# Attention's maxima on a ring of four single banks, and key tiles shared out anew for the row sums

## The reference

```python
h = _ada_ln(x, cond, Wln1, bln1)
q, k, v = heads(h @ Wq + bq), heads(h @ Wk + bk), heads(h @ Wv + bv)
scores = einsum('bhqd,bhkd->bhqk', q, k) / sqrt(32)
attn = softmax(scores, axis=-1)
x = x + (einsum('bhqk,bhkd->bhqd', attn, v) reshaped) @ Wo + bo
h = _ada_ln(x, cond, Wln2, bln2)
x = x + gelu(h @ W1 + b1) @ W2 + b2
```

## Time and profile before

| | |
|---|---|
| median of three runs | 3452.63 us (3442.79 to 3455.45) |
| the profiled execution | 3454.36 us, its span 3453.1 us |
| busy over the span: PE, DVE, ACT, POOL | 96%, 58%, 41%, 42% |
| mean granted clock of PE | 0.978 of full speed |
| reductions of maxima in attention (L382) | 983, mean 1220 ns |
| adds on POOL (L791) | 192 of 4698 ns and 32 of 4576 ns |
| transfers into `accd` | 224 of 1024 KB |

### The profile page before, as it was taken

How to read it: one execution, slowest core, us unless ns; L and a number is a source line. 1 busy time by engine, 2 the same in 40 slices (tenths; PEclk the granted TensorE clock), 3 DMA queues, 4 the chain that set the end, 5 groups by cost and what they waited for, 6 DMA issues and landing times.

```text
span 3453.1 us, 43212 instructions
## 1 busy us (share of the span) xinstructions
PE 3312.9 (96%) x16794; PEld 2157.7 (62%) x16794; DVE 2008.8 (58%) x2541; ACT 1400.0 (41%) x2739; POOL 1466.8 (42%) x662
## 2 busy tenths in 40 slices
PE   8899999999999999999999997899999999999999
PEld 7677544445454454444444542778888888778888
DVE  4547767767677676777767771843333332226666
ACT  2121456656566565666656664311111111112222
POOL 0200667667676676767667675410000000002222
PEclk9999999999999999999999998999999999989999
DMA  5474567777877877778787766921111111201221
GB/s 196 142 221 136 148 173 174 182 176 175 192 178 171 184 171 175 183 173 185 172 188 179 176 153 161 310 72 37 37 37 37 37 37 52 86 33 61 71 74 56
DMA packets 186163, 466.20 MB, mean 135 GB/s; under 512 B 27076, under 2 KB 69308, under 8 KB 154215
## 3 DMA queue, kind: packets, MB, share of 16 engines
q0 software_dynamic: 32256, 234.90, 29.6%
q1 hardware_dynamic: 153703, 228.54, 22.2%
HBM read 151.94 MB, written 75.76 MB: 66 GB/s over the span
## 4 chain that ended last, share of the span: by engine, by line
PE 75%; DMA 13%; POOL 5%; DVE 3%; issue 2%; ACT 1%; SPq 0%; POOLq 0%; DVEq 0%; ACTq 0%
DMA accd<-pt 11%; PE ps L1089 10%; PE ps L1078 10%; PE ps L366 10%; PE ps L631 10%; PE ps L643 9%; PE ps L443 4%; POOL pacc L791 4%; PE ps L1609 3%; PE ps L649 3%; PE ps L1622 3%; PE ps L447 2%; PE ps L1642 2%; PE ps L1439 1%; PE ps L951 1%
## 5 line engine op out<-in xcount | busy, mean ns | idle before, releaser
L382 DVE TENSOR_REDUCE nmp<-ps 128x2 f32<-128x1024 f32 x983 | 1150.5, 1220 | 270.5 <-PE ps L366 269.5
L703 ACT ACTIVATE pt<-ps 128x512 f32<-128x512 f32 x2048 | 1037.5, 625 | 661.5 <-PE ps L631 656.2
L791 POOL TENSOR_TENSOR pacc<-pacc,pt 128x2048 f32<-128x2048 f32 x192 | 901.9, 4698 | 97.8 <-ACT pt L703 97.7
L631 PE MATMUL ps<-qs,ks 128*128 128x512 f32 x2048 | 781.3, 415 | 2.3 <-ACT pt L703 2.3
L366 PE MATMUL ps<-ks,qs 96*128 96x512 f32 x1966 | 749.5, 422 | 5.9 <-POOL ones L767 3.3
L366 PEld LDWEIGHTS ps<-ks,qs 96*128 96x128 f32 x1966 | 352.9, 189 | 297.3 <-DVE nmp L382 200.7
L631 PEld LDWEIGHTS ps<-qs,ks 128*128 128x128 f32 x2048 | 385.7, 189 | 205.7 <-ACT pt L703 144.3
L643 PE MATMUL ps<-pt,vq 128*32 128x512 f32 x4096 | 492.3, 598 | 0.0
L1078 PE MATMUL ps<-hpb,w 128*128 128x512 f32 x1536 | 383.0, 399 | 3.3 <-DMA x_d<-x 3.3
L1089 PE MATMUL ps<-w,gp 128*128 128x512 f32 x1536 | 380.5, 396 | 2.5 <-DVE gp L1222 2.5
L1089 PEld LDWEIGHTS ps<-w,gp 128*128 128x128 f32 x1536 | 289.4, 188 | 71.8 <-DVE gp L1222 2.9
(11 more groups left out here) (168 smaller groups left out, 3211.1 us busy)
## 6 DMA issues: line engine op xcount, KB each, us to landing
accd<-pt POOLq DMA_DIRECT2D x224, 1024.0 KB, 8.8
qk_d<-st SPq DMA_DIRECT2D x128, 256.0 KB, 2.7
ks<-qk_d SPq DMA_DIRECT2D x24, 1024.0 KB, 12.4
qs<-qk_d SPq DMA_DIRECT2D x96, 256.0 KB, 6.3
xina<-in_x SPq DMA_DIRECT2D x8, 1024.0 KB, 6.6
v_d<-vst SPq DMA_DIRECT2D x32, 256.0 KB, 2.4
vq<-v_d SPq DMA_DIRECT2D x8, 1024.0 KB, 12.2
recb<-r_d SPq DMA_DIRECT2D x32, 256.0 KB
```

The source lines that it names most:

```text
L382: dve.tensor_reduce(nmp[:, n // 4, n % 4:n % 4 + 2], ps[:, bank:bank + 2, :], AX.X, ALU.max, negate=True).then_inc(s_mr, 1)
L631: pe.matmul(ps[:, n % 3, :], ksb[w % 2][:, hh, 128 * kt:128 * kt + 128], qsb[:, v % 3, hh, :], start=True, stop=True).then_inc(s_sc, 1)
L703: act.activation(pt[:, g % 8, hh, :], ps[:, n % 3, :], ACT.Exp, scale=SCALE).then_inc(s_exp, 1)
L791: pool.tensor_tensor(pacc[:, :, :], first, pt[:, g % 8, :, :], ALU.add).then_inc(s_add, 1)
```

## The change

The four shared banks become a ring of single banks. A use waits for the use four before it. Each maximum matmul is signalled on its own and reduced on its own; maxima and scores alternate strictly. Tile 2 instead of 3 and so on goes by DMA: `ADD_DMA` is 1, 2, 4, 6, 8, 10, 12 and `ADD_POOL` 0, 3, 5, 7, 9, 11, 13, 14. `pe_sums` takes tile 15, slot 1 (last tile 10), `pacc`, slot 0 (last tile 12). `pool_values` moves from behind tile 10 to behind tile 9.

```diff
--- before.py
+++ after.py
@@ -32,13 +32,9 @@
 TRI = ((0, 0), (0, 1), (1, 0))
 HG = ((0, 6), (6, 5), (11, 5))
 EARLY = 84
-ADD_DMA = (1, 3, 5, 7, 9, 11, 13)
-ADD_POOL = (0, 2, 4, 6, 8, 10, 12, 14)
+ADD_DMA = (1, 2, 4, 6, 8, 10, 12)
+ADD_POOL = (0, 3, 5, 7, 9, 11, 13, 14)
 ADD_PE = (15,)
-
-ORDER = ("m", "m", "s", "m", "s", "m", "s", "s", "m", "s", "m", "s", "s", "m", "m", "s")
-
-
 def with_maxima(ci, j):
     return ci > NCH + 1 or (ci == NCH + 1 and j >= 8)
@@ -46,9 +42,7 @@
 def max_count(v, n):
-
-    u = 64 * v + n
-    return u + 1 if u < EARLY - 2 else (EARLY - 2) + (u - (EARLY - 2)) // 2 + 1
+    return 64 * v + n + 1
 def dma_count(v, kt):
@@ -73,16 +67,16 @@
             v, f = divmod(p, 8)
             if f == 6 and v + 1 < NU:
                 self.use(("row", v + 1))
-            for i in range(4):
-                if EARLY // 2 - 1 + 4 * p + i < 32 * NU:
-                    self.use(("max", EARLY // 2 - 1 + 4 * p + i))
+            for i in range(8):
+                if EARLY - 2 + 8 * p + i < 64 * NU:
+                    self.use(("max", EARLY - 2 + 8 * p + i))
             if f == 0 and v:
                 self.use(("sums", v - 1))
         self.use(("sums", NU - 1))
     def use(self, what):
-        self.bank[what] = 3 + 2 * (len(self.uses) % 2)
-        self.before[what] = self.uses[-2] if len(self.uses) > 1 else None
+        self.bank[what] = 3 + len(self.uses) % 4
+        self.before[what] = self.uses[-4] if len(self.uses) > 3 else None
         self.uses.append(what)
@@ -342,44 +336,40 @@
             for r in range(2):
                 sp.dma_start(qsb[96 + r:97 + r, v % 3, :, :].bitcast(F32), nmr[:, r, :].bitcast(F32)).then_inc(s_md, 16)
-        def pe_pair_free(what):
+        def pe_bank_free(what):
             if ring.before[what] is None:
                 return
             kind, n = ring.before[what]
             if kind == "max":
-                pe.wait_ge(s_mr, max_count(n // 32, 2 * (n % 32) + 1))
+                pe.wait_ge(s_mr, n + 1)
             elif kind == "row":
                 pe.wait_ge(s_nh, 2 * n + 2)
             else:
                 pe.wait_ge(s_accs, n + 1)
-        def pe_max(p, half):
-            v, n = p // 32, 2 * (p % 32) + half
+        def pe_max(u):
+            v, n = divmod(u, 64)
             w = v // NCH
             hq, kc = divmod(n, 4)
             if n == 0:
                 pe.wait_ge(s_qd[v % 3], 48 * (v // 3 + 1))
                 pe.wait_ge(s_kd[w % 2], 48 * (w // 2 + 1))
-            if half == 0:
-                pe_pair_free(("max", p))
-            m = pe.matmul(ps[:, ring.bank["max", p] + half, :], qsb[0:96, v % 3, hq // 4, 128 * (hq % 4):128 * (hq % 4) + 128],
-                          ksb[w % 2][0:96, hq // 4, CH * kc:CH * kc + CH], start=True, stop=True)
-            if half:
-                m.then_inc(s_mm, 1)
+            pe_bank_free(("max", u))
+            pe.matmul(ps[:, ring.bank["max", u], :], qsb[0:96, v % 3, hq // 4, 128 * (hq % 4):128 * (hq % 4) + 128],
+                      ksb[w % 2][0:96, hq // 4, CH * kc:CH * kc + CH], start=True, stop=True).then_inc(s_mm, 1)
         def pe_row(v):
             pe.wait_ge(s_nm, v + 1)
-            pe_pair_free(("row", v))
+            pe_bank_free(("row", v))
             pe.transpose(ps[0:16, ring.bank["row", v], 0:128], nm[:, :], ident[:, :]).then_inc(s_nt, 1)
-        def dve_max(p):
-            v, n = p // 32, 2 * (p % 32)
-            bank = ring.bank["max", p]
+        def dve_max(u):
+            v, n = divmod(u, 64)
             if n == 0:
                 dve.wait_ge(s_nm, v)
-            dve.wait_ge(s_mm, max_count(v, n))
-            dve.tensor_reduce(nmp[:, n // 4, n % 4:n % 4 + 2], ps[:, bank:bank + 2, :], AX.X, ALU.max,
+            dve.wait_ge(s_mm, u + 1)
+            dve.tensor_reduce(nmp[:, n // 4, n % 4:n % 4 + 1], ps[:, ring.bank["max", u], :], AX.X, ALU.max,
                               negate=True).then_inc(s_mr, 1)
         def sp_load_k(w, r):
@@ -652,14 +642,15 @@
         def pe_sums(v):
             bank = ring.bank["sums", v]
-            pe_pair_free(("sums", v))
+            pe_bank_free(("sums", v))
             for kt in ADD_PE:
                 pe_ones(bank, pt[:, (16 * v + kt) % 8, :, :], kt == ADD_PE[0], False)
-            for i in range(2):
-                pe.wait_ge(s_dma[i], dma_count(v, ADD_DMA[len(ADD_DMA) - 1 - (len(ADD_DMA) - 1 - i) % 2]))
-                pe_ones(bank, accd[:, i, :, :], False, False)
+            pe.wait_ge(s_dma[1], dma_count(v, ADD_DMA[-2]))
+            pe_ones(bank, accd[:, 1, :, :], False, False)
             pe.wait_ge(s_add, add_count(v, ADD_POOL[-1]))
-            pe_ones(bank, pacc[:, :, :], False, True).then_inc(s_end, 1)
+            pe_ones(bank, pacc[:, :, :], False, False)
+            pe.wait_ge(s_dma[0], dma_count(v, ADD_DMA[-1]))
+            pe_ones(bank, accd[:, 0, :, :], False, True).then_inc(s_end, 1)
         def pe_attention():
             qkv_over(pe)
@@ -669,16 +660,11 @@
                 v, f = divmod(p, 8)
                 if f == 6 and v + 1 < NU:
                     pe_row(v + 1)
-                ns = nm_ = 0
-                for what in ORDER:
-                    if what == "s":
-                        pe_scores(2 * p + ns // 4, ns % 4)
-                        ns += 1
-                    else:
-                        pair = EARLY // 2 - 1 + 4 * p + nm_ // 2
-                        if pair < 32 * NU:
-                            pe_max(pair, nm_ % 2)
-                        nm_ += 1
+                for i in range(8):
+                    u = EARLY - 2 + 8 * p + i
+                    if u < 64 * NU:
+                        pe_max(u)
+                    pe_scores(2 * p + i // 4, i % 4)
                 if p:
                     pe_values(2 * p - 2)
                     pe_values(2 * p - 1)
@@ -741,12 +727,12 @@
                     dve_row_split(v + 1, ring.bank["row", v + 1])
                 if f == 1 and v:
                     dve_sums(v - 1)
-                for i in range(4):
-                    pair = EARLY // 2 - 1 + 4 * p + i
-                    if pair < 32 * NU:
-                        dve_max(pair)
-                        if pair % 32 == 31:
-                            dve_row_max(pair // 32)
+                for i in range(8):
+                    u = EARLY - 2 + 8 * p + i
+                    if u < 64 * NU:
+                        dve_max(u)
+                        if u % 64 == 63:
+                            dve_row_max(u // 64)
                 if f == 2 and v:
                     dve_recip(v - 1)
                 if v == NU - 2 and f % 2:
@@ -789,7 +775,7 @@
                         pool.wait_ge(s_add, add_count(v, kt) - 1)
                         first = pacc[:, :, :]
                     pool.tensor_tensor(pacc[:, :, :], first, pt[:, g % 8, :, :], ALU.add).then_inc(s_add, 1)
-                if kt == 10 and v:
+                if kt == 9 and v:
                     pool_values(v - 1)
             pool_values(NU - 1)
```

## The result

The changed kernel takes 3343.22 us in the median of four runs (3338.52 to 3345.59) against 3451.37 of the kernel before: ratio 0.9688, 95% interval 0.9667 to 0.9710. I had said 3313, in a range of 3298 to 3360. The direction and the mechanism were right; a little over a fifth of the forecast gain (30 of 138 us) did not arrive. The profiled execution has a span of 3341.0 us against 3453.1.

What follows compares the result with a forecast made beforehand. Attention was taken as bound by PE, with its waits inside iterations and at unit ends to be won. 76 + 66 - 2 = 140 us off 3454.36 gave 3314, stated as 3313 us for the median; range 3298 to 3360.

Steps and rivals of the forecast that it cites:

- (1): Attention iterations: single-bank ring and alternating order cut the period from 6.12 to 5.81 us, 76 us over 246 iterations.
- (a): DVE reductions in attention don't overlap, each takes its whole 0.68 us: 42 us more, 3355 us; chance 12%.
- (c): Inside iterations, waits for exponentials replace those for maxima; period stays near 6.1 us, only sums gain: 3385 us; chance 4%.
- The 0.66 us of the Trainium skill: DVE's 512-element PSUM-to-SBUF reductions: by this estimate periods some 0.08 us longer, the run about 20 us above forecast.
- (2): Turning the row and copying the sums take one ring bank instead of two; taken as 0, with 10 us for the range.
- (3): New tile sharing at unit ends: 50.5 us of idle and 12 to 14 us of halved clock go, 66 us.
- its sentence on `pool_values`: On GpSimd, `pool_values` goes one tile earlier; the recip it waits for was in place long before.
- for which I left 2: Allowance of 2 us for remnants of waits near key loads, subtracted from the forecast gain.
- 0.9 us to spare: DVE's eight reductions take 4.9 us, hidden inside a period of 5.8, with 0.9 us left.
- (b): Iteration shrinks, but sums still wait, on `pacc` behind two adds or on tile 12: 3377 us; chance 7%.
- (d): Slot 0's chain, tiles 4, 8 and 12: slow landings make tile 12 late; 3630 us at 16.0 us each; chance 3%.
- (e): PE's clock falls inside iterations; one in eight at double length adds 180 us, 3493 us; chance 2%.

Runs made afterwards that it cites:

- the runs of the two halves: Old interleaving on single banks, against the changed kernel: 3383.44 us; strict alternation on pairs of banks, against the kernel before with only the new tile sharing: 3457.68 us.

## Why the prediction was right, and where not

- **Period** (1). 5.81 us forecast, 5.77 to 5.82 measured; reductions 0.60 apart; no wait for ACT or DVE inside. The 0.66 us of the Trainium skill (VectorE: DVE Perf Modes, the section on the TRN2 errata) was not what these instructions took: 0.68 us for one alone, 0.60 from one to the next. Rivals (a) and (c) are out. With the runs of the two halves, the layout on which it rested (where a load falls due, when its bank is free) gave 6.0 to 6.1 and 6.3 to 6.5 for 6.11 and 6.41: it can be trusted to a tenth of a microsecond.
- **Row and sums on one bank** (2). I took 0. A clean unit fell by 2.94 us where eight iterations of 0.31 give 2.48, some 12 us over the run that I had not counted. The iteration with the row went from 6.36 to 5.87 us and the one with the sums from 9.69 to 9.25, the others from 6.12 to 5.79 or so: about 0.3 us a unit belongs to the row and the sums, the rest to a period slightly shorter than I took.
- **Tiles** (3). 50.5 us of idle went to 15.3, and the sums that ran at the halved clock from eight to two. The step that failed is its sentence on `pool_values`: the reciprocals were not in place long before. I had looked at when the store was issued, not at what is in flight at that moment. Its landing went from 1.4 to 6.6 us with my own moved tiles, tile 4 having just been issued. The position of `pool_values` is worth about 14 of the 27 us for which I left 2; the other 13 I put down to the chain of slot 0 beside a key load, and this is not shown.
- **What DVE has to spare** (1). "0.9 us to spare" holds for 31 units. In the one with the splits of Wo it doesn't, and I had not looked for work that happens once: 12 us.
- **A load once** (Wo) ahead of the row of maxima: 6 us. That PE waits for the row shows in the landing times; that the load of Wo holds the row up is read from the thirteen traces and was not taken away in a run.

Sum: 3313 + 27 + 12 + 6 - 12 - 2 = 3344, against 3343; the last 2 are the ones that I had left. That it closes to 1 us is in part luck: the four runs spread over 7 us, and from the last sums to the end of the span the changed kernel takes 8 us less (1324.8 instead of 1332.8), of which the last sums themselves explain about 4.5.

Rival (b) came true in a small part: seven sums still wait for `accd` (15.3 us) and five for `pacc` (4.7 us), one of my own signs of being wrong. Rival (d) seems right in its mechanism and was wrong in its extent: single landings reach 17.3 us, but the chain of slot 0 shows only in one unit of four. Rival (e) had the trace against it, and so it was: the granted clock is 1.00 over a whole clean unit (1860 to 1912 us) with eight banks used by turns in each iteration. What the Trainium skill (TensorE: Matmul & The Clock Gate, "A second HAM failure mode: psum-queue depth-cycling") says of cycling through PSUM banks does not show here: it speaks of a PE that idles often between its groups, and this one hardly stands.

The best version is the changed kernel with `pool_values` behind tile 12 and the splits of Wo in the last unit: 3317.62 us, ratio 0.9633 (0.9605 to 0.9661), the one whose interval lies clear of the changed kernel's.

## What to carry to other kernels

Lay one iteration out from the trace, with the time at which each buffer is wanted and the time at which it is free; it told this period to about 0.02 us and those of the two halves to 0.1, and that two changes of which neither shortens the period alone do it together. When you move a large transfer, look at the small ones that are issued in the microseconds after it and at who waits for them in order, for they move with it. And check a margin in the busiest iteration of the run, not in the common one.

## What the runs showed of the hardware

- A store of 8 KB issued just behind an accumulating transfer of 1 MB landed in 6.6 us in the median instead of 1.4 us when issued just ahead of one, and in 16.4 us in the run whose loads of 1 MB stand ahead of it on its own queue.
- The load of keys took 12.4 us in the median before and 17.6 after the change, with the same bytes; only what stood beside it in time had changed.
- Two adjacent adds on GpSimd in `pacc` take 9.56 us, hardly more than two apart (4.59 us each).
- The two transfers of 8 KB with the row of maxima landed in 2.8 us in the median before and 6.3 after the change, and in up to 15.9 us in the run with two key loads moved; PE's first score started 0.1 to 0.3 us after the second had landed.
